# Projections of q, k and v by tiles of tokens instead of by sequences, in a fused image and text block

## The reference

```python
h = patches @ W.T + b + pos                                  # 64 x 36 x 192
t = gelu(tok_embed[x_txt] @ W1.T + b1) @ W2.T + b2           # 64 x 32 x 192
h = concatenate([h, t], axis=1)                              # 64 x 68 x 192
x = (h - mean) / sqrt(var + 1e-5)
y = x @ fq_weight(w_qkv).T + b_qkv                           # q, k, v
y = round y to 8 bits by the smallest and the largest of all y
```

## Time and profile before

| | us |
|---|---|
| median of 3 runs | 1002.32 (1000.46 to 1004.02) |
| the profiled execution, its own time | 1000.82 |
| its span, first to last instruction | 999.0 |
| text, to the start of the loop of steps | 112 |
| loop of steps | 112 to 318 |
| extremes over all partitions, barrier | 318 to 325 |
| rounding, first scores | 325 to 424 |
| V's conversion, scalars | 424 to 449 |
| attention, second scores | 449 to 658 |
| output projection, routing, experts | 658 to 999 |

### The profile page before, as it was taken

The page is one execution under the profiler, slowest core; times in us unless marked ns, Lnnn a source line. Parts: engine busy times, 40 slices in busy tenths (PEclk is TensorE's granted clock), DMA queues, the critical chain, the costliest instruction groups (busy, mean ns, idle before and its releaser), DMA issues.

```text
span 999.0 us, 20044 instructions
## 1 busy us (share of the span) xinstructions
PE 623.0 (62%) x6502; PEld 472.7 (47%) x6502; DVE 724.1 (72%) x1719; ACT 512.8 (51%) x898; POOL 325.4 (33%) x347
## 2 busy tenths in 40 slices
PE   3599688586543377604888888734222357998950
PEld 2599577475432244402555555423122246776740
DVE  3435554767577599967999999999888754657773
ACT  3122276453531844233888888843644225887820
POOL 2022355444333121001232222220046770025575
PEclk9999698897867555555556555555555587999985
DMA  7963044221101344302222222272111323567653
GB/s 182 255 178 100 12 121 120 58 59 40 59 21 39 81 109 116 85 0 52 33 42 42 45 42 41 26 221 89 52 44 67 127 88 85 154 176 219 188 141 103
DMA packets 155152, 92.76 MB, mean 93 GB/s; under 512 B 88488, under 2 KB 147696, under 8 KB 154960
## 3 DMA queue, kind: packets, MB, share of 16 engines
q1 hardware_dynamic: 147232, 72.28, 28.0%
q0 software_dynamic: 7856, 19.68, 6.8%
HBM read 45.62 MB, written 31.85 MB: 78 GB/s over the span
## 4 chain that ended last, share of the span: by engine, by line
DVE 22%; PE 21%; issue 18%; SPq 15%; POOL 14%; ACT 5%; DMA 4%; POOLq 1%; DVEq 0%; ACTq 0%
PE ps L1702 16%; SPq L591 7%; POOL x_by_expert L752 5%; POOL R L761 3%; ACT R L768 3%; POOL R L695 2%; DVE M L1285 2%; DVE M L1286 2%; SPq L566 2%; SPq L565 2%; SPq L567 2%; POOL R L686 1%; PE ps L1969 1%; POOL R L684 1%; DVE R L1275 1%
## 5 line engine op out<-in xcount | busy, mean ns | idle before, releaser
L1702 PE MATMUL ps<-R 128*128 128x256 f16 (+6 forms) x2024 | 304.6, 307 | 48.2 <-DVE R L1659 12.9
L1702 PEld LDWEIGHTS ps<-R 128*128 128x128 f16 (+3 forms) x2024 | 222.5, 132 | 102.1 <-issue 52.4
L768 ACT ACTIVATE R<-ps 128x768 f16<-128x768 f16 (+7 forms) x257 | 178.1, 730 | 101.6 <-PE ps L1969 36.0
L1702 PE MATMUL ps<-M 32*128 32x68 bf16 (+4 forms) x1192 | 101.6, 245 | 101.7 <-DMA M<-R 69.4
L1702 PEld LDWEIGHTS ps<-M 32*128 32x128 bf16 (+3 forms) x1192 | 65.7, 116 | 153.7 <-issue 61.2
L771 ACT ACTIVATE R<-R,sc 128x512 f16<-128x512 f32 (+11 forms) x107 | 83.8, 839 | 101.9 <-DMA R<-v_rows 28.0
L768 ACT ACTIVATE R<-R 128x512 f16<-128x512 f32 (+5 forms) x145 | 74.7, 533 | 105.8 <-POOL R L686 66.6
L733 POOL TENSOR_TENSOR R<-R,M 128x884 f32<-128x884 f32 x32 | 53.2, 1664 | 147.7 <-ACT M L912 147.7
L761 POOL DMA_INDIRECT R<-y_by_tile,M x68 | 67.0, 986 | 101.0 <-DMA y_by_tile<-R 82.1
L752 POOL DMA_INDIRECT x_by_expert<-R,M x68 | 67.2, 988 | 59.7 <-DVEq L1578 39.5
L1873 PE MATMUL ps<-ident_b,R 128*68 128x128 bf16 x416 | 56.2, 308 | 20.9 <-ACT R L768 19.0
(11 more groups left out here) (279 smaller groups left out, 1130.9 us busy)
## 6 DMA issues: line engine op xcount, KB each, us to landing
R<-x_by_expert SPq DMA_DIRECT2D x41, 192.0 KB, 2.9
y_by_tile<-R SPq DMA_DIRECT2D x41, 192.0 KB, 2.6
R<-in_x_dram SPq DMA_DIRECT2D x12, 576.0 KB, 8.4
M<-R SPq DMA_DIRECT2D x16, 260.0 KB, 3.1
M<-R SPq DMA_DIRECT2D x32, 130.0 KB, 2.0
R<-w_split SPq DMA_DIRECT2D x1, 4032.0 KB, 22.7
v_rows<-R SPq DMA_DIRECT2D x16, 204.0 KB
R<-v_rows SPq DMA_DIRECT2D x16, 204.0 KB
```

What stands on the lines that cost most here:

```text
L768: return act.activation(out_, in_, ACT.Copy)
L1702: return pe.matmul(o, a, b, start=start, stop=stop, skip_group_check=True)
```

## The change

`xT` and the units of projection go by tiles instead of sequences. A unit is two text tiles (256 columns, units 0 to 7) or three image tiles (288 columns, units 8 to 15). `UNITS_AT` gives the step of each: text units 0 to 5 in steps 2 to 7, units 6 and 7 in steps 24 and 26 (their place in `yqk` holds pixels until then), image units in steps 10, 11, 16, 17, 22, 23, 25 and 28. Three image tiles are normalised in one step instead of two. `turn_x` and `x_out` come a step after `x_high` and `x_low`; `xf1` and `x16` have six places instead of four. ScalarE normalises by one activation with scale and bias (VectorE makes the bias, one instruction more in `ln_deviation`), and `by_patch` is on GpSimd alone, with all three channels. V's bias enters by a fourth product for each tile: ones (three rows) times the bias divided by V's scale, in three bf16 parts, made once by VectorE in step 0 (`v_ratio`). V's maximum comes with its scaling. `evac_qk` writes image columns to their places by sequence. V's 16 loads, on SyncE among those of q and k, become four on ScalarE's queue at the start of the next stage. `tstage`, `emb` and `wtmp` move to other places; the text rows are stored by an unrolled loop.

```diff
+        XSTEP = [k // 2 for k in range(16)] + [6 * q + 8 + w // 3 for q in range(3) for w in range(6)] + [23, 23, 23, 26, 26, 26]
+        UNITS_AT = {2: 0, 3: 1, 4: 2, 5: 3, 6: 4, 7: 5, 10: 8, 11: 9, 16: 10, 17: 11, 22: 12, 23: 13, 24: 6, 25: 14, 26: 7, 28: 15}
-        WSTEP = [6, 7, 13, 16, 19, 22]
+        WSTEP = [9, 12, 13, 18, 19, 21]
...
+            def store_v(e):
+                u = UNIT_ORDER[e]
+                sp.wait_ge(sem("v_scaled"), v_done(e + 1))
...
-            pipeline(sp, [(load_four, 0), (load_v, 0)], 16)
+            pipeline(sp, [(load_four, 0)], 16)
...
-                pool.tensor_tensor(v, h, mv[0:n, x, 0:1].to_broadcast([n, C]), ALU.subtract).then_inc(sem("centred"), 1)
-                pool.wait_ge(sem("centred"), x + 1)
-                pool.tensor_tensor(v, v, rs[0:n, 2, x:x + 1].to_broadcast([n, C]), ALU.mult).then_inc(sem("xn"), 1)
...
-            def v_bias(g):
-                pool.wait_ge(sem("v_scaled"), g * 2 + 2)
-                v = vst[:, g % 2]
-                pool.tensor_tensor(v, v, bvrow[0:N, :].unsqueeze(1).to_broadcast([N, 4, C]), ALU.add).then_inc(sem("v_stored"), 1)
...
+            def normal(x):
+                n = x_rows(x)
+                h = tstage[x] if x < 16 else hstage[:, (x - 16) // GRID % 2, (x - 16) % GRID, :]
+                act.wait_ge(sem("ln_done"), x_batch(x) + 1)
+                wait(act, "x_low", x - XR1 + 1)
+                ident_(xf1[0:n, x % XR1], h, scale=rs[0:n, 2, x:x + 1], bias=rs[0:n, 0, x:x + 1]).then_inc(sem("xn"), 1)
...
+                copy(xT[:, :, x_cols(x)], ps[:, 4, :].bitcast(F16)[:, at:at + 3 * n].rearrange("p (k t) -> p k t", k=3)).then_inc(sem("xT"), 1)
...
+                        y = y[:, 16 * q:16 * q + 16, 0:NI].rearrange("p b (h w) -> p b h w", w=GRID)[:, :, :, 3 * half:3 * half + 3]
+                        o = o[:, 0:288].rearrange("p (w b h) -> p b h w", w=3, h=GRID)
+                    ident_(y, o, scale=wscale[:, j:j + 1], bias=biases[:, 2 + j:3 + j]).then_inc(sem("qk_stored"), 1)
...
             barrier(act, "act")
+            for q in range(4):
+                act.dma_start(yv[:, 16 * q:16 * q + 16, :], v_dram[16 * q:16 * q + 16].rearrange("b n c -> n b c")).then_inc(sem("v_in"), 16)
...
+            def scale_v(e):
+                wait(dve, f"v_saved{e % 2}", v_stores(e))
+                for k, tiles_ in enumerate(v_items(u)):
+                    dve.wait_ge(sem("v_psum"), v_done(e) + k + 1)
+                    dve.tensor_tensor_reduce(out=vst[0:n, e % 2, 2 * k:2 * k + m], in0=ps[0:n, item_bank(e, 3 + k), 0:m * C].rearrange("p (i c) -> p i c", i=m),
...
+                    for j in range(3):
+                        qk = y[:, j, 16 * q:16 * q + 16, 0:NI].rearrange("p b (h w) -> p b h w", w=GRID)[:, :, :, 3 * half:3 * half + 3]
+                        dve.tensor_reduce(ext[:, 0, col:col + 1], qk, mybir.AxisListType.XYZ, ALU.max)
+                        dve.tensor_reduce(ext[:, 1, col:col + 1], qk, mybir.AxisListType.XYZ, ALU.min)
...
+                        mm(o, hi, wqT0[:, 2 * C:3 * C], True, False)
+                        mm(o, lo, wqT0[:, 2 * C:3 * C], False, False)
+                        mm(o, both, wqT1[:, 2 * C:3 * C], False, False)
+                        last = mm(o, ones_three[:, 0:m], bv_three, False, True)
```

292 lines of the change are left out of this document (158 added, 134 removed).

## The result

The kernel after the change took 968.01 us (median of 4 runs, 961.94 to 971.55), the kernel before, run beside it, 1001.39. The ratio is 0.9658, with a 95% interval from 0.9604 to 0.9712: faster by 3.4%, 33 us. The forecast was 946, so 22 us are missing. The profiled execution took 968.72 us, its span is 966.7; I had forecast 944.0 for it.

A forecast was written before the change was run, and what follows sets the result against it. A ring of waits among GpSimd, ScalarE, TensorE and VectorE was taken to bound the 206 us loop. 1000.82 less 53.5 (loop) and 3.3 (V's return) gave 944.0 profiled, 945.5 as median, say 946; range 923 to 978.

The forecast's parts named there:

- Dear scatter: Rival: image q and k copies out of PSUM cost 2.1 us each, +22 us, 968; chance 0.24 shared with slow hand-offs.
- slow hand-offs: Rival: in-order queues lose 20% rather than 5%, or a V store is held, +22 to +30, 970; shared chance 0.24.
- V's return: Stage after the loop: V's loads as four on ScalarE's queue; gain 6.65, losses 1.4 and 2, net 3.3 us less.
- The contention: First q and k load meets V's 3.3 MB in flight: 0 to 4 us lost, taken as 2.
- The gain of 6.65: After the loop: VectorE's 6.65 us wait, with V's last load late, goes away, and no more is gained.
- The loop's 53.5 us: Loop over image and text tiles, 112 to 318 us: 206 us becomes 152.5, 53.5 less.
- the tail: Loop from step 24 on, followed as one chain to the last unit's reductions: 21 us.
- 7 us for hand-offs: Allowance of 5% on top of the loop's 145.5 us for engines handing work to each other.
- A loss of half a microsecond for six units done: Steps 0 to 7 with six text units in steps 2 to 7: 40.5 us, against 40 before.
- The rule that I had weighed against the change: Full speed needs successive accesses in one 16-byte line, PSUM's lines are 8 bytes; so scatter moves to PSUM, not away.
- The ring: Mid-loop waits passing between GpSimd, ScalarE, TensorE and VectorE, through V's bias and normalising on GpSimd; one turn 10.5 us.
- Off the ring: Bias and normalising leave GpSimd, whose remaining copies and six differences of weights then hold up no turn of the loop.

The follow-up runs named there:

- each part alone: Two runs on the kernel before: V's bias by a product of three rows, 984.13 us (0.9838); ScalarE's normalising, 974.89 us (0.9754).

## Why the prediction was right, and why it was not

The range (923 to 978) held the time, and the direction with its chance of 0.94 was right. The forecast of 946 missed by 22 us, and the case that came about is none of my rivals. Dear scatter had 968 as its time, but there was no such scatter. So it is luck that the range held: its upper part stood for scatter and slow hand-offs, and V's loads, at which I had put 3.4 us, filled it with 33.7.

**The step that failed** is in V's return: "Loss: four issues before ScalarE's conversion, on the path, 0.31 to 0.79 each: 1.4." They took 29.06. The rows that I took the price from are issues of 204 KB, one at a time, a whole load of q and k apart; that is what an issue takes when little is queued. I had even worked out that 3.3 MB would be in flight, but charged it only to the first q and k load. No issue in the trace of before was a warning: the stores of V, 204 KB from 68 partitions too, take 0.30 us each and stand 10.5 us apart.

```profile
193.19 0.30 SPq L544 DMA_DIRECT2D v_rows<-R  x1
...
203.73 0.29 SPq L544 DMA_DIRECT2D v_rows<-R  x1
```

The sign was elsewhere, and I didn't look: while the first of these stores moved, from 193.8 to 196.8, the DMA share was 0.23, a rate of 66 GB/s. That is a quarter of the engines, as in the 29 us after.

The contention that I put at 2 us was 4.6, over the 4 that I had named as what would make the forecast wrong. The gain of 6.65 was there: V is converted without a wait, and the line "to the scale of the row maxima" has -8.4.

**The loop's 53.5 us** came out to a tenth, and the tenth is chance: the same loop ends anywhere from 258.63 to 264.76 in seven profiles. The terms are right one by one only within 5 us. Steps 0 to 7 took 44.8 us (40.5), steps 8 to 23 82.3 (84), the tail 25.6 (21), where the forecast kept 7 us for hand-offs apart; with these spread in proportion it had 42.5, 88 and 22, so it was 2.3 and 3.6 short and 5.7 over. Single steps were further off: step 9 took 2.8 us (6.7), step 15 9.7 (4.2). "A loss of half a microsecond for six units done" was wrong: step 8 began at 147.4 before and begins at 156.8 now, 9.4 us later. The sum didn't hang on it, since it was made against the whole stage of 206. The last two marks are in TensorE's timeline (the first is at 156.77):

```profile
233.51 0.71 PE L1819 MATMUL ps<-ident,R 96*128 96x96 f32 x6
...
239.12 2.40 PE L1757 MATMUL ps<-R 3*96 3x192 bf16 x13
```

Step 23 begins at 233.51 (near 232 forecast), step 24 at 239.12. The prices behind it, by shape, 112 to 265 us:

```profile
L792 ACT ACTIVATE R<-ps,biases,M 128x288 f32<-128x288 f32 x24 | 13.7, 649 | 6.2 <-PE ps L1757 6.1
L792 ACT ACTIVATE R<-ps,biases,M 128x256 f32<-128x256 f32 x24 | 12.0, 574 | 1.2 <-PE ps L1757 1.1
...
L792 ACT ACTIVATE R<-M,R 96x192 f32<-96x192 f32 x24 | 11.3, 536 | 8.7 <-DVEq L1197 8.7
L1273 DVE TENSOR_REDUCE R<-R 128x1 f32<-128x288 f32 x24 | 10.7, 444 | 0.7 <-DVE R L1170 0.6
...
L789 ACT ACTIVATE R<-ps 128x288 f16<-128x288 f16 x24 | 8.1, 409 | 7.9 <-PE ps L1836 7.7
```

- Image q and k out of PSUM: 0.65, not 1.1, and hardly more than a straight 256 at 0.574. There is hardly a scatter price in runs of three fp32. The rule that I had weighed against the change (the Trainium skill, SBUF — State Buffer, the note on cachelines) would have this PSUM read, at a stride of 96, and the write pay for each line; of PSUM the page says it for matmuls, and I had stretched it to ScalarE. The trace doesn't bear that out here, and it made me give "dear scatter" more of a chance than the rows did.
- Normalising 0.54, not 0.45; reductions of 288 0.44 and turned image rows 0.41, as forecast (0.45, 0.42).
- Bias products 0.21 to 0.31, not 0.09: 8.6 us in all, not 3.6. In a step with a text unit this is the whole miss: 5.50 us (steps 4 to 7) against 5.1. Steps 2 and 3 took 8.2 and 7.4, and TensorE's granted clock from 112 to 130 was 0.69, where I had put 1.0 for these steps.
- So errors cancelled: image copies were too dear by 24 x 0.45, or 11 us of ScalarE's time, and bias products too cheap by 5 us of TensorE's. How much of the rest is hand-offs, and how much VectorE's stalls (last section), wasn't taken apart. The forecast had no term for those stalls, neither before, where two of them cost the chain 8.9 us over their usual time, nor after, where four cost 7.4.

**The ring** was read rightly as far as its names go: both of GpSimd's waits are gone, and each part alone made the loop shorter. "Off the ring" was too simple, though. With GpSimd out and the rows turned in the same step, TensorE still waited 30.1 us for VectorE's low parts, and it took the step's delay (7 us at the least) on top of both. That this turn closes through ScalarE, whose high parts stand behind its copies of q and k, is my reading; no run took that link away alone.

**Not foreseen:** 3.5 us before GpSimd's reduction over partitions. Before, it came 3.69 us behind VectorE's last reduction, with 5.84 of idle issue on GpSimd, as with normalising on ScalarE alone (5.81). Wherever GpSimd had been idle for 30 us ahead of it, it followed within 0.2. What GpSimd does in the 5.8 us isn't shown. With the bias alone gone from GpSimd the 3.5 us are gone too (0.18).

## What to carry to other kernels

A load's issue is cheap only while its queue has room, so before a load is put on the queue of an engine with work on the path, work out how long all bytes ahead of it take, at the rate of as many DMA engines as its partitions allow; 68 partitions ran on a quarter of them, and 64 plus 4 on all. Loads that have time go into the same queue behind those that have none, since another queue frees an engine but not the way. And when a sum comes out right, take it apart all the same: here two parts that looked like two ways to open one ring were worth 13 and 23 us, and the gain of both together is a third short of the whole.

## What the runs showed of the hardware

**A load that stalls its engine.** 29 to 36 us for four issues on ScalarE, with DMA at 0.27 and the engine at rest. On all DMA engines the same bytes ran at 176 GB/s and not at four times 79. What stands ahead of the issue isn't held: seven conversions of ScalarE ran beside an issue of 6.34 us that follows them in the program.

**VectorE's small instructions beside GpSimd.** Instructions of six columns, 0.17 us as a rule, take ten times that where they meet GpSimd's difference of weights, and end with it:

```profile
180.27 2.37 POOL L722 TENSOR_TENSOR R<-R 128x1152 f16<-128x1152 f32 x1 [7.69 <-ACT R L789]
```

```profile
180.48 2.19 DVE L1170 TENSOR_SCALAR R<-R 96x6 f32<-96x6 f32 x1
...
185.93 1.84 DVE L1177 TENSOR_TENSOR R<-R 96x6 f32<-96x6 f32 x1
```

GpSimd's instruction ends at 182.64 and VectorE's at 182.67; the next pair, from 185.38 and 185.93, at 187.74 and 187.77. Both are on the chain that ended last in the changed kernel, twice each, and over 0.17 they cost it 7.4 us. The change didn't bring this. Before, GpSimd ran V's bias, a patch copy and the difference one behind the other from 177.49 to 182.16, and VectorE stood through all three (again at 222.59), on the chain too:

```profile
177.54 4.64 DVE L1154 TENSOR_TENSOR R<-R 96x6 f32<-96x6 f32 x1
```

To keep the difference of weights away from these instructions is a next thing to try; no run here took it away.

**Short products of another kind.** A product of three rows in bf16 between products of 128 rows in fp16 costs 0.31 us in a step at the full clock (5.50 against 4.87, two of them), where one of the twelve of V takes 0.10; two of them side by side cost 0.13 each (5.14). That it is the turn between the two kinds that costs was shown by the order alone; what in the turn costs, rows or type, wasn't taken apart.
